# Stores of the result issued by ScalarE's queue behind each copy, in a fused window-attention and axial-attention kernel

## What is computed

```python
x = x + _L0_conv_ref(_gn(x), ...)   # group norm; shifted 8x8-window attention, 16 heads, cosine logits, position bias
x = x + _L1_conv_ref(_gn(x), ...)   # group norm; attention without softmax along the columns, and along the rows, summed
return x                            # (32, 16, 16, 256), float32
```

## Time and profile before

| | us |
|---|---|
| median of three runs | 896.25 (895.89 to 896.89) |
| the profiled execution | 903.6 |
| its span on the core | 901.4 |
| TensorE busy | 844.6 (94%) |
| VectorE busy | 736.4 (82%) |
| ScalarE busy | 662.7 (74%) |
| GpSimd busy | 480.2 (53%) |

### The profile page before, as it was taken

How to read it: one execution, slowest core, us unless ns; L and a number is a source line. 1 busy time by engine, 2 the same in 40 slices (tenths; PEclk the granted TensorE clock), 3 DMA queues, 4 the chain that set the end, 5 groups by cost and what they waited for, 6 DMA issues and landing times.

```text
span 901.4 us, 45971 instructions
## 1 busy us (share of the span) xinstructions
PE 844.6 (94%) x20128; PEld 659.9 (73%) x20128; DVE 736.4 (82%) x1536; ACT 662.7 (74%) x1108; POOL 480.2 (53%) x358
## 2 busy tenths in 40 slices
PE   5477899999999999999999999999999999999876
PEld 3354677778788777778787777778777778787655
DVE  7879888888889888888898888888888888887452
ACT  3656777877777778777777787777877877777542
POOL 4445455665655555655655556565565655654220
PEclk9699999999999999999999999999999999999988
DMA  6101434343344443343444443334444343334453
GB/s 165 58 13 36 80 75 81 66 88 78 80 83 92 92 91 82 84 82 81 81 89 92 89 84 81 78 79 87 88 91 92 77 87 77 74 72 94 78 108 83
DMA packets 334430, 74.04 MB, mean 82 GB/s; under 512 B 282372, under 2 KB 333718, under 8 KB 334230
## 3 DMA queue, kind: packets, MB, share of 16 engines
q1 hardware_dynamic: 322128, 69.53, 37.2%
q10 hardware_dynamic: 12102, 1.59, 1.1%
HBM read 12.31 MB, written 8.40 MB: 23 GB/s over the span
## 4 chain that ended last, share of the span: by engine, by line
PE 76%; SPq 7%; DVE 6%; issue 4%; ACT 3%; DMA 2%; POOL 1%; ACTq 1%; DVEq 0%; POOLq 0%
PE ps L559 20%; PE ps L629 15%; PE ps L672 8%; PE ps L661 6%; PE ps L650 6%; PE ps L576 4%; PE ps L662 3%; PE ps L600 3%; PE ps L591 3%; PE ps L609 3%; SPq L439 3%; SPq L429 2%; PE ps L714 1%; PE ps L708 1%; DMA gram_wide<-gram 1%
## 5 line engine op out<-in xcount | busy, mean ns | idle before, releaser
L1372 POOL TENSOR_TENSOR kv<-kv,kv 128x1024 f16<-128x1024 f32 x60 | 128.6, 2144 | 87.1 <-ACT kv L1018 84.3
L1082 ACT ACTIVATE probs<-probs 128x1024 f32<-128x1024 f32 x64 | 67.8, 1059 | 89.5 <-DVE probs L1660 87.4
L1377 POOL TENSOR_TENSOR stat<-stat,small 128x2 f32<-128x2 f32 x64 | 43.3, 693 | 135.5 <-DVE stat L1568 127.8
L661 PEld LDWEIGHTS ps<-q,gram_wide 128*128 128x128 f16 x2048 | 107.2, 97 | 10.9 <-DVE probs L1660 4.9
L661 PE MATMUL ps<-q,gram_wide 128*128 128x32 f16 x2048 | 111.3, 176 | 3.2 <-DMA gram_wide<-gram 2.6
L662 PE MATMUL ps<-q,gram_wide 128*128 128x16 f16 x2048 | 110.4, 169 | 0.0
L662 PEld LDWEIGHTS ps<-q,gram_wide 128*128 128x128 f16 x2048 | 106.0, 97 | 0.4
L559 PE MATMUL ps<-xn,w_q 128*128 128x256 f16 x768 | 98.3, 279 | 6.5 <-POOL xn L1372 6.5
L1594 DVE SCALAR_TENSOR_TENSOR gram<-ps,small,gram 128x512 f16<-128x512 f32 x128 | 94.6, 794 | 8.0 <-ACT gram L1035 5.1
L1372 POOL TENSOR_TENSOR xn<-xn,xn 128x512 f16<-128x512 f32 x64 | 74.9, 1171 | 48.7 <-ACT xn L1071 48.7
L1035 ACT ACTIVATE gram<-ps,small 128x512 f16<-128x512 f32 x128 | 95.4, 818 | 4.4 <-PE ps L650 4.4
(11 more groups left out here) (124 smaller groups left out, 1976.4 us busy)
## 6 DMA issues: line engine op xcount, KB each, us to landing
gram_wide<-gram SPq DMA_DIRECT2D x248, 128.0 KB
v_wide<-kv SPq DMA_DIRECT2D x496, 32.0 KB
x_in<-x SPq DMA_DIRECT2D x32, 128.0 KB, 2.4
x_in<-x SPq DMA_DIRECT2D x64, 64.0 KB, 2.3
out<-y_out SPq DMA_DIRECT2D x32, 128.0 KB
out<-y_out SPq DMA_DIRECT2D x64, 64.0 KB
gram_wide<-gram ACTq DMA_DIRECT2D x8, 128.0 KB
x<-L_conv_w_qkv SPq DMA_DIRECT2D x1, 768.0 KB, 4.5
```

What stands on the lines that cost most here:

```text
L661: pe.matmul(dst.rearrange("p (t i) -> p t i", t=2), high, q1[a][:, :, cols], start=True, stop=False)
L1082: act.activation(part, part, ACT.Exp).then_inc(probs_ready[g], 1)
L1372: return pool.tensor_tensor(dst, whole, high, ALU.subtract)
L1377: pool.tensor_tensor(stat[layer][:, 28:30], stat[layer][:, 26:28], minus_half, ALU.pow).then_inc(gn_pow[layer], 1)
```

## The change

The three DMAs of a store are issued by ScalarE's queue in place of SyncE's, each directly behind `result_copy` of the same image, both in the loop and in the tail. The bytes, pieces, buffers and semaphores of a store stay the same. All 32 stores move; SyncE keeps its last wait for them.

```diff
@@ block.sync, step(k) @@
                 for img in there(k - 6):
                     spread_v_rows(0, img)
                     spread_v_rows(1, img)
-                for img in there(k - 10):
-                    store_image(img)
                 for img in there(k - 6):
                     spread_gram(0, img)
@@ block.sync, tail @@
             spread_v_rows(1, pic[28])
-            store_image(pic[24])
             spread_gram(0, pic[28])
-            store_image(pic[25])
             spread_v_rows(0, pic[29])
...
             spread_gram_front(1, pic[30])
-            store_image(pic[26])
             spread_gram_front(0, pic[30])
             spread_v_front(0, pic[31])
             spread_v_front(1, pic[31])
-            store_image(pic[27])
             spread_gram_front(0, pic[31])
             spread_gram_front(1, pic[31])
-            store_image(pic[29])
-            store_image(pic[28])
-            store_image(pic[30])
-            store_image(pic[31])
@@ block.scalar @@
+            def store_image(img):
+                reach(act, y_copied, img)
+                for src, dst in pieces(out_rows[img.n], y_out[:, img.par]):
+                    act.dma_start(dst, src).then_inc(stored[img.par], 16)
@@ block.scalar, step(k) @@
                 for img in there(k - 6):
                     result_copy(img)
+                    store_image(img)
                 for img in there(k - 1):
                     probabilities(0, img)
@@ block.scalar, tail: the same line behind each result_copy @@
             result_copy(pic[26])
+            store_image(pic[26])
             q1_high(1, pic[29])
...
             result_copy(pic[27])
+            store_image(pic[27])
             o1_side(0, pic[29])
             spread_v_back(0, pic[30])
...
             result_copy(pic[28])
+            store_image(pic[28])
             result_copy(pic[29])
+            store_image(pic[29])
             o1_side(0, pic[31])
...
             result_copy(pic[30])
+            store_image(pic[30])
             result_copy(pic[31])
+            store_image(pic[31])
```

More of the change, by code:

```diff
@@ L254, in build @@
         gram_hi = [sem(f"gram_hi{a}") for a in range(2)]
+        gram_first = [sem(f"gram_first{a}") for a in range(2)]
         gram_lo = [sem(f"gram_lo{a}") for a in range(2)]
@@ L456, in spread_gram_front, with store_front @@
                                  gram[a][rows].rearrange("p s e t -> p s (e t)")).then_inc(gram_spread[a], 16)
-            def store_image(img):
+            def store_front(img):
                 reach(sp, y_copied, img)
-                for src, dst in pieces(out_rows[img.n], y_out[:, img.par]):
+                for src, dst in pieces(out_rows[img.n], y_out[:, img.par])[:2]:
                     sp.dma_start(dst, src).then_inc(stored[img.par], 16)
@@ L1037, in gram_high, with store_back, gram_high_of @@
                 last.then_inc(gram_hi[a], 1)
+            def store_back(img):
+                reach(act, y_copied, img)
+                for src, dst in pieces(out_rows[img.n], y_out[:, img.par])[2:]:
+                    act.dma_start(dst, src).then_inc(stored[img.par], 16)
+            def gram_high_of(head, a, img):
+                if head == 0:
+                    reach(act, gram_done[a], img)
+                    reach(act, gram_spread[a], previous(img), 64)
+                act.activation(gram_half(a, head, 0), gram_psum(a, head, img), ACT.Copy,
+                               scale=gram_mask[:, head:head + 1]).then_inc((gram_first, gram_hi)[head][a], 1)
             def spread_v_back(a, img):
@@ L1601, in o1_sum, with gram_low_of @@
                                   along(o1_32[a][:], 1), ALU.add).then_inc(o1_summed[a], 1)
+            def gram_low_of(head, a, img):
+                if head == 0:
+                    dve.wait_ge(gram_first[a], 1)
+                    reach(dve, o1_done[a], previous(img))
+                else:
+                    reach(dve, gram_hi[a], img)
+                last = dve.scalar_tensor_tensor(gram_half(a, head, 1), gram_psum(a, head, img), gram_mask[:, head:head + 1],
+                                                gram_half(a, head, 0), ALU.mult, ALU.subtract)
+                if head == 1:
+                    last.then_inc(gram_lo[a], 1)
             def o1_low(a, img):
```

## The result

The changed kernel takes **910.38 us**, median of five runs (907.48 to 912.01), beside 896.89 us (895.89 to 899.93) for the kernel before in the same comparison: a ratio of 1.0138, 95% interval 1.0113 to 1.0164. The forecast said 898.35, at most 901.0. Its sign was right, its size was not: it had 2.1 us more, and by the ratio 12.4 came (10.1 to 14.7).

What follows compares the result with a forecast made beforehand. The prediction took TensorE to bound the loop, with little hiding anything in the tail. G -0.4, C +0.1, A +1.0, D +1.4 and F 0 gave +2.1 us on the median 896.25, thus 898.35 us, range 895.4 to 901.0.

Steps and rivals of the forecast that it cites:

- What bounds the kernel: Loop: TensorE is the bound; SyncE's queue has 1.2 us to give by the wait table, 4.9 at most.
- Price of a store: Three DMA issues on ScalarE's queue cost as on SyncE's: 1.8 us clean, 2.2 mean, plus 0 to 0.1 wait.
- Loop, ScalarE's side: Loop: the 2.92 us gap before the exponentials covers a store's issues, so they cost nothing; 1.8 us an image without it.
- G: Loop, SyncE's side: gain from stores leaving SyncE's queue ahead of gram_wide, between -1.2 us and 0, taken -0.4.
- DMA traffic: Loop: a store's 256 KB travelling beside gram_wide transfers could hold TensorE by some tenths; taken 0.
- C: Tail, store 26: ScalarE's idle time of 1.92 us nearly covers it; cost 0 to 0.2 us, taken 0.1.
- A: Tail, store 27: delays ScalarE's following work by 1.9 us, partly given back on SyncE's queue; 0 to 1.9, taken 1.0.
- D: Tail, stores 28 and 29: o1_side(0) and the last chain wait for the issues; 1.4 us, ends 1.0 and 2.7.
- F: Tail, clock under the last axial_y: more idle ahead could change its speed; between -1.8 and +0.7 us, taken 0.
- (a): Rival, loop and tail: full give-back, with A 0.3, G -0.8, D 1.0; +0.6 us, 896.9; chance 0.34.
- (b): Rival, loop: SyncE's queue is the hidden bound, so TensorE's 4.9 us idle returns; -2.4 us, 893.85; chance 0.09.
- (c): Rival, loop and tail: queues exclude each other, a store takes 3.7 us and ScalarE spills over; +9, 905; chance 0.05.

Runs made afterwards that it cites:

- e9: Changed kernel's loop stores issued by ScalarE one stage later, in front of o_high, with the tail's stores on SyncE's queue: 899.19 us, 1.0000 to the kernel before.
- e0: The kernel before, unchanged, profiled a second time in one execution: 897.82 us.
- e1: Kernel before, all stores left on SyncE's queue, plus three small ScalarE DMAs (4 KB in all) behind each copy of the loop: 909.24 us, 1.0105.
- e8: Kernel before, with only the first of each loop store's three DMAs issued by ScalarE behind the copy, the others and the tail by SyncE: 900.47 us, 1.0006.
- e5: Kernel before, with only the tail's stores (images 26 to 31) moved to ScalarE's queue: 901.01 us, 1.0005.
- a0: The changed kernel again, unaltered, timed beside later runs: 910.92 us, 1.0113 to the kernel before.
- e13: Changed kernel, with SyncE waiting for the scores before its v_wide issues, so that only ScalarE issues during them: 919.62 us.
- e7: Kernel before, with TensorE's wait in front of axial_out(1) on VectorE's first biased score in place of the second: 899.14 us, 0.9987.
- e14: Kernel before, with SyncE waiting for the scores before its v_wide issues, so that no queue issues during them: 916.24 us.
- e3: Changed kernel, with ScalarE in the loop waiting for the scores before it issues a store: 921.97 us, 1.0234 to the kernel before.

## Why the prediction was wrong

- **What bounds the kernel**: right. TensorE bounds the loop; taking the loop's stores off SyncE's queue was worth nothing (e9: 1.0000).
- **Price of a store**: right, and somewhat high. Over the loop's 26 stores the median is 1.53 us, with 0.02 us of wait, where the sum had 1.8 clean, 2.2 as a mean, and 0 to 0.1.
- **Loop, ScalarE's side: "The cost is nothing, with this gap as the cover."** This is the step that failed. The gap covered all that was asked of it: the exponentials never waited for the issue. But the step counted only what is queued behind the issue on its own engine. It didn't look at what TensorE does in the 1.7 us of the issues, which are the scores. Their result comes 0.41 us later in the median (1.63 against 1.22), and VectorE's biased scores have nothing to spare before `axial_out`, which already waited for them. Cost: 0.37 us an image, 9.5 us. The rows of before had what it takes to see the place, though not the price. In the step of the earlier trace rows, with the copy's end at 411.29:

```profile
411.69 0.95 PE L591 MATMUL ps<-qk,k_two 32*128 32x64 f16 x96
```

- **Loop, SyncE's side, G = -0.4**: not shown, and small in any case. The wait for `gram_wide` is 0.4 us after, 1.2 in the first profile of before and 0.7 in e0; e9 has the same relief and measured 1.0000.
- **DMA traffic, taken 0**: right; e1 has almost the full cost without the moved bytes, e8 none with half of them.
- **Tail, C + A + D = +2.5**: too high for what e5 measures (+0.5, with the +2.5 just outside its upper bound of 2.3), though the profiles of single executions put the tail at more, and the mechanisms show in the profile of after:

```profile
854.93 2.29 ACTq L1062 DMA_DIRECT2D out<-y_out  x3
857.33 0.60 ACT L1068 ACTIVATE o<-ps 128x512 f32<-128x512 f32 x1 [2.42 <-issue]
...
892.74 1.49 ACTq L1062 DMA_DIRECT2D out<-y_out  x3
894.33 0.60 ACT L1068 ACTIVATE o<-ps 128x512 f32<-128x512 f32 x1 [1.62 <-PE ps L653]
```

  Store 27 delays what is behind it, by 2.3 us; TensorE's wait behind that chain, 0.51 us in the earlier trace rows, is 1.6 us after and 1.2 us in e5. `o1_side(0)` of image 31 begins 1.62 us behind the copy of image 29, directly at store 29's end (894.23), where it began 0.99 us behind it before: 0.6 us late. Both stores were clean, 1.55 and 1.49 us, where the sum had 2.2 as the mean. The same 0.6 us stand in front of the last `axial_y`, which waits 3.3 us for VectorE where it waited 2.70. So D was 0.6 in this execution, and in e5's, and not 1.4; in a0's, where store 29 took 2.91 us, the same wait was 5.5 us, 2.8 more than before. F, taken 0, holds: the last `axial_y` took 4.24 us after, beside 4.46 and 4.10 in e0.
- **Rivals**: (a) and (b) are out. (c) is out for the change: of the 26 stores in the loop one took 3.37 us, the others at most 2.29. A cost of its sign and rough size (its +9 us) came about in another place, which the prediction had no rival for. The rule of the Trainium skill (Perfetto Trace Analysis, DMA Instruction — HWDGE), a descriptor generator locked for one sequencer at a time, was set beside rival (c), which priced a store at 3.7 us. The traces show no such price: a store takes 1.53 us in the median beside SyncE's busy queue (after) and 1.52 us when SyncE issues nothing at that time (e13). Whether sharing of that kind is behind the lag can't be told from these runs.

One profile alone can't price the tail: the part behind the loop's 26 steps is 91.6 us in after and 88.4 in e0, but also 91.8 in the first profile of before, 89.7 in e7 and 88.4 in e1, which all have the tail of before. What stays open is by which path an issue delays the scores' result. Shown is that it does, where, and how much.

## What to carry to other kernels

A DMA issue can cost more than its time on its own engine: lay its interval over the timeline of the engine that bounds the kernel, and see whether a result that is waited for without slack is being made in it. Here this was a run of small matmuls, with another queue issuing already. The same three issues made each image 0.37 us longer (1.4%) in one gap of ScalarE and cost nothing in another. And a queue's share of the chain of waits isn't a gain to be had until the wait table of the bounding engine names that queue.

## What the runs showed of the hardware

- DMA issues on SyncE's or ScalarE's queue delay the result of a run of 96 small matmuls (32x64, with their weight loads, 0.9 us long). From the run's start to the reader's start: 1.03 us with no issue (e14), 1.20 with one queue issuing (before, e13), 1.45 to 1.64 with both. Of the growth from one queue to both, a part stands in the matmuls (0.08 of 0.30 us in e1, 0.14 of 0.35 after, by the means), the rest between the last of them and the reader's start.
- The size of the DMA hardly enters: 4 KB in three issues (1.53) count nearly as much as 256 KB in three (1.63); 128 KB in one issue that ended before the scores count nothing (1.20).
- Three issues of the same store took 1.53 us in the median behind the copy and 2.4 us when issued some 1.6 us later (e3). What makes the difference was not looked into.
- Two queues that issue side by side did not lengthen each other's issues: 1.53 us for a store on ScalarE's queue with SyncE issuing (after), 1.52 without (e13).
